# Second phase: row maxima twelve steps ahead of the scores instead of fourteen, with the output products and one value product on other steps

## What is computed

```python
q1 = jnp.einsum('bshd,hed->bshe', qh, wq1)
k1 = jnp.einsum('bshd,hed->bshe', kh, wk1)
q2, k2 = ...                                   # the same with wq2, wk2
vp = jnp.einsum('bshd,hed->bshe', vh, wv)
s1 = jnp.einsum('bshe,bthe->bhst', q1, k1) / scale
s2 = jnp.einsum('bshe,bthe->bhst', q2, k2) / scale
attn = jax.nn.softmax(s1, axis=-1) - gain * jax.nn.softmax(s2, axis=-1)
o = jnp.einsum('bhst,bthe->bshe', attn, vp)
mean = jnp.mean(o, axis=-1, keepdims=True)
var = jnp.mean(jnp.square(o - mean), axis=-1, keepdims=True)
o = (o - mean) / jnp.sqrt(var + EPS)
out = o.reshape(B, S, D) @ wo.T
```

## Time and profile before

| | |
|---|---|
| median of 3 runs | 1506.55 us (1506.32 to 1508.69) |
| the profiled execution | 1507.06 us, its span 1505.2 us |
| granted TensorE clock over the span | 0.999 |
| busy: PE, PEld | 1472.3 us (98%), 1042.9 us (69%) |
| busy: DVE, ACT, POOL | 1140.7 us (76%), 846.5 us (56%), 389.5 us (26%) |
| second phase, first to last exponential | 349.5 to 806.6 us |
| costliest group: DVE line 1655, row maxima | 256 times, 307.5 us, 1219 ns each |
| ACT line 1599, exponentials | 256 times, 262.4 us, 1025 ns each |

### The profile page before, as it was taken

The page is one execution under the profiler, slowest core; times in us unless marked ns, Lnnn a source line. Parts: engine busy times, 40 slices in busy tenths (PEclk is TensorE's granted clock), DMA queues, the critical chain, the costliest instruction groups (busy, mean ns, idle before and its releaser), DMA issues.

```text
span 1505.2 us, 28685 instructions
## 1 busy us (share of the span) xinstructions
PE 1472.3 (98%) x11017; PEld 1042.9 (69%) x11017; DVE 1140.7 (76%) x2307; ACT 846.5 (56%) x1123; POOL 389.5 (26%) x416
## 2 busy tenths in 40 slices
PE   9999999999999999999999999999999999999998
PEld 5333343435666666666656888898989898898987
DVE  6445544369899999999967888788786878778686
ACT  5888899976888888888863431222222231222221
POOL 1000000124548766666453420000000000000001
PEclk9999999999999999999999999999999999999999
DMA  7756656556756656656652201110010101100001
GB/s 151 148 103 116 114 116 125 92 103 114 109 82 107 105 79 110 111 74 98 93 175 71 77 15 29 26 32 15 22 36 15 36 22 29 27 26 20 20 24 29
DMA packets 89887, 108.91 MB, mean 72 GB/s; under 512 B 18244, under 2 KB 58192, under 8 KB 89752
## 3 DMA queue, kind: packets, MB, share of 16 engines
q1 hardware_dynamic: 89624, 106.90, 37.4%
q10 hardware_dynamic: 128, 0.20, 0.0%
HBM read 26.29 MB, written 4.19 MB: 20 GB/s over the span
## 4 chain that ended last, share of the span: by engine, by line
PE 82%; DVE 7%; SPq 3%; ACT 3%; issue 2%; DMA 1%; POOL 1%; POOLq 0%; DVEq 0%; ACTq 0%
PE ps L109 78%; SPq L119 3%; PE ps L1431 2%; ACT H L683 1%; ACT PX L1599 1%; PE ps L1393 1%; PE ps L1439 1%; DVE NM L1655 1%; DVE EE L850 1%; DMA ST<-QS 0%; POOL X L1832 0%; PE ps L1364 0%; DVE GH L2528 0%; DVE GF L2524 0%; DVE QS L757 0%
## 5 line engine op out<-in xcount | busy, mean ns | idle before, releaser
L1655 DVE TENSOR_REDUCE NM<-ps 128x4 f32<-128x1024 f32 x256 | 307.5, 1219 | 24.3 <-PE ps L109 23.0
L1599 ACT ACTIVATE PX<-ps 128x1024 f32<-128x1024 f32 x256 | 262.4, 1025 | 76.2 <-PE ps L109 74.3
L683 ACT ACTIVATE H<-ps,b1c 128x1024 f32<-128x1024 f32 x256 | 267.7, 1119 | 38.4 <-PE ps L109 37.0
L2299 ACT ACTIVATE GF<-ps,cols 128x512 f32<-128x512 f32 x128 | 87.2, 687 | 216.9 <-PE ps L109 199.1
L109 PE MATMUL ps<-XC,W_sw_w 128*128 128x512 f32 x768 | 187.1, 393 | 0.0
L109 PEld LDWEIGHTS ps<-XC,W_sw_w 128*128 128x128 f32 x768 | 140.1, 188 | 27.5
L2647 POOL TENSOR_SCALAR RSc<-AGc 128x4 f32<-128x4 f32 x23 | 6.1, 263 | 576.3 <-DVE AGc L2414 576.3
L2294 ACT ACTIVATE GF<-ps 128x512 f32<-128x512 f32 x64 | 38.2, 596 | 183.8 <-PE ps L109 183.8
L2530 DVE TENSOR_TENSOR GH<-GF,GH 128x512 fp32r<-128x512 f32 x192 | 133.2, 694 | 6.6
L109 PE MATMUL ps<-PX,VT 128*32 128x256 f32 x2048 | 137.0, 385 | 0.6 <-DVE X L1640 0.4
L109 PE MATMUL ps<-KT,QT 48*128 48x512 f32 x512 | 127.5, 495 | 2.0 <-DVE NM L1655 0.9
(11 more groups left out here) (252 smaller groups left out, 2509.6 us busy)
## 6 DMA issues: line engine op xcount, KB each, us to landing
KT<-KS SPq DMA_DIRECT2D x128, 192.0 KB, 4.7
ST<-QS SPq DMA_DIRECT2D x254, 96.0 KB, 2.8
QT<-XSb SPq DMA_DIRECT2D x128, 96.0 KB, 4.2
XR<-TT SPq DMA_DIRECT2D x352, 32.0 KB, 1.9
XT<-in_xT_dram SPq DMA_DIRECT2D x8, 512.0 KB, 3.9
raw_a<-in_x_dram SPq DMA_DIRECT2D x8, 512.0 KB, 4.2
CR<-in_ctxT_dram SPq DMA_DIRECT2D x8, 512.0 KB, 6.3
out_dram<-X SPq DMA_DIRECT2D x7, 512.0 KB, 2.9
```

What stands on the lines that cost most here:

```text
L683: e.activation(H1[s % 8][:, :, :], PP[s % 3][:, :, :], ACT.Tanh, bias=b1c[:, half:half + 1], scale=1.0).then_inc(act_th, 1)
L1599: e.activation(PX[s % 3][:, :, :, :], PP[2][:, :, :].rearrange("p g (c q) -> p g c q", c=2), ACT.Exp, bias=0.0, scale=0.25).then_inc(act_e ...
L1655: e.tensor_reduce(NM[u % 2][:, qc, :, :, i], PP[qc][:, :, :].rearrange("p g (m k) -> p g m k", m=2), AX.X, ALU.max, negate=True).then_inc( ...
L2299: e.activation(g[:, :], o, f, bias=cols[:, col:col + 1], scale=1.0).then_inc(act_g, 1)
```

## The change

`LEAD` goes from 14 to 12: maxima and their reductions come two steps later, from step -12 to step 243. `rows_due` (-5 to -3) and SP's put (-4 to -2) follow, so that rows stand on step 5 of eight and puts on steps 6 and 14 of sixteen, behind load(i=1) of step 12. The two halves of an output product, which stood on steps 41 + 8b and 45 + 8b, stand together on 41 + 8b; DVE adds both in one operation. The third quarter of a pair's values goes from step -3 to -5 (29 to 27 of 32, for p = 1 too), the first of all from -11 to -10. `BUSY` loses three filler matmuls, `LAST_W2` goes from -13 to -11.

```diff
-LAST_W2 = -13
+LAST_W2 = -11
...
-LEAD = 14
-SECOND_VALUES = (25, 29, 31, 33)
+LEAD = 12
+SECOND_VALUES = (25, 27, 31, 33)
...
-BUSY = {-11: 3, -10: 1, -9: 1, -8: 1, -7: 1, -6: 1, -5: 1, -4: 2, -3: 1, -2: 1}
+BUSY = {-10: 1, -9: 1, -8: 1, -7: 1, -6: 1, -5: 1, -4: 2, -3: 1, -2: 1}
...
     def v_due(s):
-        for i, at in enumerate((-17, -7, -3, -1)):
+        for i, at in enumerate((-17, -7, -5, -1)):
...
-        return (0, 0) if s == -11 else None
+        return (0, 0) if s == -10 else None
...
         for b in range(2):
-            for qc in range(2):
-                p = due(s, 41 + 8 * b + 4 * qc, 32, NP - 1)
-                if p is not None:
-                    return p, b, (qc,)
+            p = due(s, 41 + 8 * b, 32, NP - 1)
+            if p is not None:
+                return p, b, (0, 1)
...
     def rows_due(s):
-        return due(s, -5, 8, NU)
+        return due(s, -3, 8, NU)
...
-            u = due(s, -4, 8, NU)
+            u = due(s, -2, 8, NU)
             if u is not None:
                 put_maxima(u)
```

## The result

The kernel after takes 1541.4 us (1540.9 to 1552.4) against 1506.7 for the kernel before on the same chip: 1.0245 times as long, 95% interval 1.0226 to 1.0264. The forecast was 1521, the range ended at 1538: the sign was right, the size was not.

A forecast was written before the change was run, and what follows sets the result against it. The loop of scores and exponential was taken to bound the second phase. Outputs +7.9, rows -1.6, value product +3.2, puts +6 and start -1 gave +14.5 us on 1506.55, so 1521 us; range 1507 to 1538.

The forecast's parts named there:

- The bound and the method: Second phase: a closed loop of scores and exponential, 1.62 to 1.67 us a step; PE time counts only where a step outlasts it.
- Outputs: Both halves of an output product on steps 9 and 17: +0.61 us each, 13 times, +7.9 us (bounds +5.6, +10).
- Rows: Row transposes leave the key product's step, 3 of every eight: 1.70 us for 1.76, 27 times, -1.6 us (bounds 0, -3.8).
- Value product: Moved from step 29 to 27, seven times: -1.4 us in step 29, +4.6 in step 27, net +3.2.
- In the steady part nothing: Maxima twelve ahead: no steady cost, since banks, waits and order between a maxima product and its reduction stay.
- Puts in the steady part: Row-maxima transfers on SP, with two steps less lead, land late before a block's first scores: +6 us (bounds 0, +22).
- rival B: Row-maxima puts land in time, so their 6 us drop out: 1515 us, 1510 to 1516; chance 0.20.
- The fold: End of the phase: maxima 254 and 255 go to steps 242 and 243, before the fold: nothing.
- Start: First scores of the second phase: 3.0 us gained by less DVE work, SP takes two: -1 us (bounds -6, +2).
- The clock: Full in every stretch read; the three filler matmuls removed stood in idle PE time and cost nothing.
- Rival C: Puts land behind the load's data, 16 stalls of 1.1 us and more: 1537 us, 1527 to 1540; chance 0.14.
- The sign, slower: Whole kernel: slower with chance 0.78, same 0.12, faster 0.10.

## Why the prediction was wrong, point by point

- **The bound and the method: right.** Steps of 1.62 to 1.67 us with priced excesses give the steady part: forecast 8.6 us without the puts, measured 7.5, of which 1.2 are one put.
- **Outputs: right, mis-sized.** +7.9 for 13. Step 9 is 2.68, not 2.87: the 0.91 was taken whole for the second six, but twelve matmuls in a row take 1.67 us (433.95, PE) where six take 0.96 (422.43 in the kernel before), so the second six add 0.71, and the step rose by 0.72. Step 10 is 1.92, not 1.85; step 18 rose by only 0.15, since it had stood at 1.77. 12 of them cost 6.0 in the kernel after, 5.3 alone.
- **Rows: right in sign, too small.** 0.06 us each was forecast, 0.14 measured (step 3: 1.76 to 1.62; 18 in the stretch, -2.5). The answer to the earlier trace rows in the kernel after, where the key product's step now ends with the loop and not with ACT:

```profile
594.12 1.03 ACT L1598 ACTIVATE PX<-ps 128x1024 f32<-128x1024 f32 x1 [0.17 <-PE ps L109]
595.04 0.59 ACT L1588 ACTIVATE KS<-ps 128x512 fp32r<-128x512 f32 x1
595.74 1.02 ACT L1598 ACTIVATE PX<-ps 128x1024 f32<-128x1024 f32 x1
```

  The bound of 0.14 was in the text; the value taken, from a drained key product, was the wrong end.
- **Value product: the sum near, its parts wrong.** +2.7 was forecast for six, and steps 25 to 31 cost +4.0. That this is near is luck. Step 27 rose by 0.27 instead of 0.65. Step 29 rose by 0.2 instead of falling by 0.2, in large part by VectorE's work; the 1.83 of the earlier trace rows was one case, the mean was 1.92. And 1.2 of the 4.0 are the one put below. "In the steady part nothing" was the failed sentence: the split's place among the other steps' work depends on the lead modulo eight, and VectorE's spare 3.7 us in 50 are a mean.
- **Puts in the steady part: +6 forecast, 1.2 measured.** 23 of 24 cost nothing, which is rival B's case. The put of row block 17 is issued at 598.71 and the scores run at 601.84, 0.1 us after the exponential that they need anyway ends (600.71 + 1.02):

```profile
601.84 0.33 PEld L109 LDWEIGHTS ps<-QT,KT 52*128 52x128 f32 x4 [0.26 <-DMA QT<-NR]
```

  Step 7 stays at 1.71. The 3.01 us left between the put's start and the scores were right (598.71 to 601.73), and the put was there by 601.84; the 2.49 us landing came from a crowded queue and wasn't the nearest case. The one exception is the put of row block 28, the last pair's first. Its rows are ready at 755.51, a load keeps SP until 755.8, the two issues take 2.38 us where those of block 17 took 1.43, and the second lands 2.29 later:

```profile
759.84 0.30 PEld L109 LDWEIGHTS ps<-QT,KT 52*128 52x128 f32 x4 [1.44 <-DMA QT<-NR]
```

  That step takes 2.87 us for 1.71. It alone is the rise of the mean of step 31. The fixed cost of about 2.0 us that the forecast took from the Trainium skill ("DMA: Bandwidth & Descriptors", "Anatomy of one DMA") is given there for DMAs that GpSimd issues, and these go through SP; they landed after 2.26 us (scores 0) and 2.29, and after 4.11 and 4.99 behind other loads.
- **The fold: a step left out, 12 us and 2 to 4 behind it at the lower clock.** This is the largest failed step. The part on the maxima went through the queue that the put passes, and named load(i=1) and one context load. That was the steady pattern; `load_fold` on step 228 is issued once, ahead of the put, and stands in no steady block. One put of 32 cost more than the whole steady part. The rule of the Trainium skill that the forecast had weighed ("DMA: Bandwidth & Descriptors", "Queues, rings and completion order", descriptors consumed in ring order on each engine) agrees with this place: the put landed 4.99 us after its issue behind sixteen DMAs of weights, and 4.45 in the run with the fault put into the kernel before. But 8.9 of the 12 us were SP's issuing (from 769.92, when the rows were ready, to 778.83), which that rule doesn't speak of.
- **Start: -1 forecast, +11.7 measured, beyond the bound of +2.** Two steps of DVE's time had been taken as a gain, of which SP would eat two thirds. SP's order in the prologue wasn't worked through with times: put 0 moved behind load(1, 1), 4.3 us later, and put 2 behind load(2, 1).
- **The clock: no term, about 9 us.** The text said that it is full in every stretch read, and so it was. In the kernel after, TensorE stood still for 5.3, 2.8 and 12.2 us, and when it went on it ran at 0.50 for another ten, ten and six us. The Trainium skill says so ("TensorE: Matmul & The Clock Gate", "HAM oscillation — how this bites in real kernels": a wait for a DMA lets the engine be throttled again, and the work behind it starts cold); trace and runs agree. The forecast priced a wait at its length.
- **Rival C** came nearest, 1537 and up to 1540 for 1541.4, by the wrong mechanism: sixteen stalls of a us, where there were three of 3 to 12 us and one of 1 us at places that occur once.
- **The sign, slower, was right** for reasons that hold only in part: of the 14.5 us forecast some 5 (outputs, rows, step 27) came from where they were reasoned to come, and 27 of the 35 lie in the start, the fold and the clock behind them.

## What to carry to other kernels

When an instruction moves on a queue, list what it passes on every step at which it is issued, the prologue and the end with their one-time loads among them, and not in one steady block. A wait of TensorE that lasts several us can cost more than its length, for the clock behind it (about 9 us here on 20 of waits). A cover of filler matmuls kept the clock, but it must be shorter than the wait; of the two kinds tried in the same place, that of 48 rows lost the clock and that of 128 kept it. And where a wait moves when its releaser is issued earlier, ask for the engine's whole work in these steps, and for the bank's users as well as the engine's time.

## What was not expected of the hardware

- The granted clock fell to 0.50 while TensorE was 100% busy with fillers of 48 of 128 rows (767 to 776 us, 1.00 to 0.58 to 0.50), and stayed at 1.00 with fillers of 128 rows in the same place. Which property of the matmuls decides was not tried further.
- The first 32 steps differ from run to run: the shift at exponential 32 was 11.7, 13.2 and 15.2 us in three kernels with the loads and puts of the kernel after, but 5.2 to 7.3 in the five in which the extra fillers stood before scores 0 and 16. Two kernels with one code up to exponential 40 had 1.8 and 8.0: in the second a put came late for scores 8, TensorE waited 2.0 us for it (0.7 in the first), and the clock was 0.50 some us later.
